# Channel attention: one product for numerator and denominator, paired row groups, rings of three banks

## The chip, the cores and the metric
The kernel runs on one NeuronCore of a Trainium2 chip. The metric is the device time of one execution in microseconds. The engines named here are TensorE (PE; PEld is its weight load), VectorE (DVE), ScalarE (ACT), GpSimd (POOL) and SyncE (SP, which only issues DMAs). PE writes to PSUM, which has eight banks of 512 float32 columns on 128 partitions.

## The reference, cut to what matters
The program is a decoder of twelve stages in float32 on x of shape (16, 128, 256): 16 batch elements of 128 tokens with 256 channels. Each stage is `x = layernorm(x + f(x))`. Stages 8 and 11 of the twelve are channel attention, and the change is in these two. The second multiplies the result by gamma.

```
def _L2_xattn_ref(q, k, v):          # x, ctx_2048, ctx_2048
    N_HEAD = 8
    qh = q.reshape(b * h, d // h, m)      # a head is 16 tokens; m = 256 channels
    kh = k.reshape(b * h, d // h, -1)
    vh = v.reshape(b * h, c // h, -1)
    qk = jnp.einsum('bdm,bdn->bmn', qh, kh) * scale       # 256 x 256 per head
    sm = jax.nn.softmax(qk, axis=-1)
    ret = jnp.einsum('bmn,bcn->bcm', sm, vh)
x = _layernorm(x + _L2_xattn_ref(x, ctx_2048, ctx_2048), axis=-1)
```

So for each of 16 batch elements and 8 heads there is a 256 by 256 softmax whose inner dimension is 16.

## The kernel before, in words
Every engine runs its own list of instructions in order, and semaphores (the `Signal` objects, `wait_ge` and `then_inc`) join them. A stage is a class; `Channels` is the first of the two, `ChannelsGamma` the second, with the same code. `Channels.order` (a generator) gives the order of steps to all engines: a loop over turns t, in which the steps work on different batch elements b, so that the stage is a pipeline over the 16 elements. Each engine's method goes through `order` and does its own share of a step.

The steps for one batch element b are these.
- "vt": PE turns the context (L2867, two 128 by 128 transposes), ACT copies it out as V (L2930), and POOL makes of it two masked copies VE, one for the even heads and one for the odd (L3023). POOL also makes XE (L3014) and KE (L3017), x and the context with the other heads' rows scaled to zero (parity e), and with one row of KE that lets a later constant be added.
- "s": PE computes scores (L2878) to find the largest of each row. A head pair lies on one group of 32 partitions, so a matmul has 32 rows, and four such matmuls can stand on the array's four row groups. The step is done for each half k of the 256 rows, into banks 0 to 3, and DVE takes the largest (L2967, four reductions).
- "sh": PE turns the largest values (L2887) and DVE puts them into the spare rows of XE (L2973). It uses bank 7, as "vt" does.
- "t": PE computes the scores again, turned and with the largest subtracted (L2899), four steps k on two row groups each, into banks 4 and 5; ACT takes the exponential (L2937) into E.
- "o": PE multiplies E with VE (L2912, hVE, the numerator, 16 matmuls) and then with ones masked in the same way (L2912, hone, the denominator, 8 and 8 matmuls), in four column groups, into bank 6. ACT copies the bank out (L2943).
- "mul": DVE takes the reciprocal over the full width of 256 columns (L2979), multiplies (L2982 or L2984) and adds x (L2987).
- "stats", "rsqrt", "scale": the layer norm of a group of four batch elements on DVE (`moments_of`, `rsqrt_of`, `scale_vector`).
- "aside": steps of the stage that comes next, placed in this stage's turns. For the second channel attention they belong to Quant (weights rounded; L2410, L2415 on PE in bank 7, L2516 to L2522 on DVE), in turns 3 to 16.

`room[n]` holds for each PSUM bank the signal that PE has to wait for before it writes the bank again. A float32 matmul shows in the trace as two records, so a step of 8 matmuls is "x16".

Of the kernel before, what the change touches and what calls it, by code (L numbers as in the profile page):

```python
# [2796 lines left out]
class Channels(Stage):  # L2797
# [6 lines left out]
    def weights(self):  # L2804
        c = self.c
        self.ctx, self.par, self.row, self.rp, self.gm = (
            c.f32("hctx", NB, D), c.f32("hpar", 2), c.f32("hrow", 2), c.f32("hrp", 2, 128), c.f32("hgm", 1))
# [6 lines left out]
    def load(self, sp):  # L2814
# [5 lines left out]
        self.fetch(sp, 4, (self.rp[:, :, :], i["c_rowpar"]), (self.gm[:, :], i["h_gamma"]))  # L2820
# [3 lines left out]
    def buffers(self):  # L2824
        c = self.c
        self.KE, self.XE, self.VE, self.V, self.MX, self.E, self.O = (c.sets(n, "h" + m, *z) for n, m, *z in (
            (3, "KE", 2, D), (3, "XE", 2, D), (3, "VE", 2, 2, 128), (2, "V", 2, 128), (2, "MX", 2, 128), (2, "E", 8, 2, D), (2, "O", 2, D)))
        self.R, self.P1 = [c.R, c.f32("hR", 4, D)], c.f32("hone", 2, 128)
        t, s, v, p = ((lambda name, n, e=e: self.sig(e, name, n)) for e in ("tensor", "scalar", "vector", "gpsimd"))
        self.ct, self.sc, self.sh, self.tr, self.o = t("ctx", 16), t("scores", 32), t("largest", 16), t("turned", 64), t("out", 16)  # L2830
        self.vk, self.ex, self.oc = s("v", 16), s("exp", 64), s("out", 16)
        self.row1, self.mx, self.xs, self.mul, self.sum = v("row", 1), v("max", 32), v("shift", 16), v("mul", 16), v("sum", 16)
        self.xe, self.ke, self.ve = p("xe", 16), p("ke", 16), p("ve", 16)
# [4 lines left out]
    def order(self):  # L2838

        yield "vt", 0, 0  # L2840
        for t in range(NB + 3):
            for step, b, k in (("sh", t - 1, 0), ("s", t, 0), ("mul", t - 3, 0), ("t", t - 1, 0), ("o", t - 2, 0), ("t", t - 1, 1), ("s", t, 1),
                               ("o", t - 2, 1), ("t", t - 1, 2), ("vt", t + 1, 0), ("o", t - 2, 2), ("t", t - 1, 3)):
                if 0 <= b < NB:
                    yield step, b, k
                if step == "s" and k == 1:
                    for n, first in (("stats", 6), ("rsqrt", 7), ("scale", 8)):
                        if t >= first and (t - first) % 4 == 0:
                            yield n, (t - first) // 4, 0
                    if t in self.ASIDE:  # L2850
# [762 lines left out]
```

## Time and profile before

| | us |
|---|---|
| median of 3 runs | 4110.23 |
| the three runs | 4107.7, 4110.23, 4121.14 |
| span of the profiled execution | 4117.8 |
| DVE busy in it | 3057.9 |
| ACT busy in it | 1939.7 |

The span is the time from the first to the last instruction of the one execution that was profiled; it lies within the range of the three runs' times. PE busy time is that of matmuls whose ends are modelled, so a busy PE is not a PE at its peak. Where an engine's row ends in square brackets, they say how long it had been idle before and who released it.

### The profile page before, as it was taken

To read this page: it belongs to the slowest core of one execution; us is meant where nothing else is said; L and a number is where in the kernel's file an instruction comes from. 1 tells how busy PE (TensorE), PEld (TensorE's weight loads), DVE (VectorE), ACT (ScalarE), POOL (GpSimd) and SP (SyncE) were. 2 spreads that over 40 slices of the span, in tenths; PEclk is the share of its full clock that TensorE was granted. 3 is DMA by queue.
4 is the path that set the end of the run, shared out by engine and by line. 5 is a ranking of instruction groups with operands and counts; after the bars stand their busy time and mean duration, and the time that the engine had idled before them with its cause. 6 is when DMAs were issued, how large, how long until landed. Compare 5 with 4: busy or idle time off the path is not lost. (4 is left out here: it accounts for less than half of the span.)

```text
span 4117.8 us, 65960 instructions
## 1 busy us (share of the span) xinstructions
PE 3583.7 (87%) x23747; PEld 2223.2 (54%) x23762; DVE 3057.9 (74%) x6508; ACT 1939.7 (47%) x4746; POOL 1167.6 (28%) x1208
## 2 busy tenths in 40 slices
PE   7799999998981777879999979888999999997885
PEld 3466666665661345645455545465655656564543
DVE  7788988988658675543455657868988898885678
ACT  4466666665532333311333324435656656563445
POOL 2533213334302000000111122114656555553210
PEclk9899999999995888889899988999999999997877
DMA  2222222222200100020000000022212211221000
GB/s 70 65 66 67 60 62 65 66 56 56 61 14 31 34 1 24 2 76 1 22 1 1 1 31 2 27 92 83 77 68 77 72 72 72 67 79 63 2 1 21
DMA packets 240594, 185.94 MB, mean 45 GB/s; under 512 B 117648, under 2 KB 216592, under 8 KB 239184
## 3 DMA queue, kind: packets, MB, share of 16 engines
q1 hardware_dynamic: 240272, 181.73, 14.7%
q8 instruction: 192, 3.15, 0.3%
q14 instruction: 130, 1.06, 0.1%
HBM read 166.45 MB, written 15.20 MB: 44 GB/s over the span
## 5 line engine op out<-in xcount | busy, mean ns | idle before, releaser
L310 PE MATMUL ps<-xT,min 128*128 128x512 f32 (+1 forms) x1072 | 503.0, 614 | 30.7 <-DVE macc L3349 30.3
L3349 DVE SCALAR_TENSOR_TENSOR macc<-ps,mcw,macc 128x508 f32<-128x508 f32 (+2 forms) x408 | 302.1, 741 | 81.2 <-ACT macc L3276 71.3
L3431 POOL TENSOR_TENSOR mSQ<-mSQ,mtn 128x512 f32<-128x512 f32 x128 | 240.2, 1877 | 362.1 <-ACT mtn L3301 362.0
L310 PEld LDWEIGHTS ps<-xT,min 128*128 128x128 f32 (+1 forms) x1072 | 191.9, 191 | 250.6 <-issue 204.3
L3424 POOL TENSOR_TENSOR mE<-mE,mCB 128x1024 f32<-128x1024 f32 x128 | 302.3, 2362 | 44.5 <-DVE mE L3359 26.5
L3359 DVE TENSOR_TENSOR_SCAN mE<-mE,mid 128x1024 f32<-128x1024 f32 x128 | 296.9, 2319 | 0.0
L3209 PE MATMUL ps<-mwo,macc 128*128 128x256 f32 x1024 | 244.5, 382 | 5.4 <-DVE macc L3366 5.3
L2937 ACT ACTIVATE hE<-ps 128x512 f32<-128x512 f32 x256 | 139.0, 595 | 223.5 <-PE ps L2899 223.5
L2351 POOL TENSOR_TENSOR lP<-lP,lm 128x512 f32<-128x512 f32 x64 | 66.6, 1041 | 574.5 <-DVE lm L2324 574.5
L3297 ACT ACTIVATE mtn<-ps,mcol 128x64 f32<-128x64 f32 x1024 | 222.9, 334 | 2.9 <-PE ps L3188 2.8
L826 POOL TENSOR_TENSOR dTB<-did,dNB 128x1024 f32<-128x1024 f32 (+1 forms) x10 | 28.7, 2869 | 662.6 <-DMA dNB<-d_N 598.4
L2260 ACT ACTIVATE lP<-ps,lm 128x128 f32<-128x128 f32 x256 | 90.6, 366 | 266.1 <-DVE lm L2320 266.1
L2967 DVE TENSOR_REDUCE hMX<-ps 128x2 f32<-128x512 f32 x256 | 158.8, 683 | 58.8 <-PE ps L2878 58.7
L3209 PEld LDWEIGHTS ps<-mwo,macc 128*128 128x128 f32 x1024 | 186.1, 192 | 28.7 <-DVE macc L3366 8.2
L732 DVE SCALAR_TENSOR_TENSOR dav<-ps,dsmall,dav 128x508 f32<-128x508 f32 (+2 forms) x192 | 142.3, 741 | 46.7 <-ACT dav L603 42.1
L2899 PE MATMUL ps<-hXE,hKE 32*128 32x256 f32 x1024 | 165.3, 445 | 12.9 <-DVE hXE L2973 7.9
L831 POOL TENSOR_TENSOR dTB<-dTB,dtmp 128x30 f32<-128x30 f32 (+11 forms) x300 | 168.7, 562 | 23.5
L732 DVE SCALAR_TENSOR_TENSOR daq<-ps,dsmall,daq 128x508 f32<-128x508 f32 (+2 forms) x192 | 142.3, 741 | 42.5 <-ACT daq L603 37.0
L830 POOL TENSOR_TENSOR dtmp<-dNB,dTB 128x30 f32<-128x30 f32 (+11 forms) x300 | 155.9, 520 | 23.5
L732 DVE SCALAR_TENSOR_TENSOR dak<-ps,dsmall,dak 128x508 f32<-128x508 f32 (+2 forms) x192 | 142.1, 740 | 25.3 <-ACT dak L603 20.7
L502 PE MATMUL ps<-dKQ 128*128 128x256 f32 x512 | 138.3, 397 | 25.9 <-ACT dO L678 17.3
L2161 PE MATMUL ps<-lCQ,lq 128*128 128x512 f32 (+1 forms) x256 | 142.6, 656 | 17.8 <-DVE lQA L2315 17.8
(581 smaller groups left out, 8470.9 us busy)
## 6 DMA issues: line engine op xcount, KB each, us to landing
mE<-m_decay SPq DMA_DIRECT2D x128, 512.0 KB, 3.6
dwk<-in_L_attn_Wk SPq DMA_DIRECT2D x64, 128.0 KB, 2.3
dwq<-in_L_attn_Wq SPq DMA_DIRECT2D x64, 128.0 KB, 2.4
dwv<-in_L_attn_Wv SPq DMA_DIRECT2D x64, 128.0 KB, 2.4
dwg<-in_L_attn_Wg SPq DMA_DIRECT2D x64, 128.0 KB, 2.4
dwo<-in_L_attn_Wo SPq DMA_DIRECT2D x64, 128.0 KB, 2.6
min<-in_m_in SPq DMA_DIRECT2D x2, 4096.0 KB, 18.5
d_N<-dNT SPq DMA_DIRECT2D x256, 16.0 KB, 1.5
```

Of the source, the lines that this page charges most:

```text
L310: t = pe.matmul(out, w[:, j, :], self.c.xT[:, j, blk(g, 512)], start=j == 0, stop=j == 1)
L732: x = dve.scalar_tensor_tensor(out=acc[:, :, 3 - j:T], in0=p[:, :, 0:T - 3 + j], scalar=small[:, 4 * k + j:4 * k + j + 1], in1=acc[:, :, 3 ...
L830: then(pool.tensor_tensor(part, bc(NB[:, s, s + 1:32], s, True), bc(TB[:, s, 0:s], 31 - s), ALU.mult))
L831: then(pool.tensor_tensor(low, low, part, ALU.subtract))
L2899: t = pe.matmul(bank(4 + i)[:, blk(lt, 256)], self.KE[x][r, e, blk(lt)], self.XE[x][r, e, :], start=True, stop=True)
L2967: m = dve.tensor_reduce(self.MX[y][:, k, 32 * r:32 * r + 32:16], bank(r).rearrange("p (e n) -> p e n", e=2), AX.X, ALU.max, negate=True)
L3209: t = pe.matmul(bank(to + j // 2)[:, blk(j % 2, 256)], self.acc[s][:, blk(j)], self.wo[:, i, :], start=i == 0 and j % 2 == 0, stop=i == 31 ...
L3297: x = act.activation(self.tn[s][:, h], bank(6)[:, h], ACT.Copy, scale=self.col[:, 4 * g + j, 2 * i + e:2 * i + e + 1])
L3349: x = dve.scalar_tensor_tensor(out=acc[:, :, 3 - j:T], in0=p[:, :, 0:T - 3 + j], scalar=self.cw[:, i, j:j + 1], in1=acc[:, :, 3 - j:T], op ...
L3359: dve.tensor_tensor_scan(E, E, self.id8[:, :, :].rearrange("p b t -> p (b t)"), 0.0, ALU.mult, ALU.add).then_inc(*self.de.up)
L3424: pool.tensor_tensor(E, E, bc(self.CB[g % 2][:, :, :].rearrange("p b t -> p (b t)"), 2), ALU.mult).then_inc(*self.em.up)
L3431: pool.tensor_tensor(self.SQ[g % 2][:, :], self.SQ[g % 2][:, :], self.tn[s][:, :], ALU.add).then_inc(*self.sqa.up)
```

## The change
It rewrites the stage's steps and their order.
- "vt" writes V straight into VE, 32 columns for each head pair and parity: 16 of V and 16 that are set to one at the stage's start. So "o" is one product of 16 matmuls whose output has the numerator on 16 partitions and the denominator on the next 16. POOL does nothing for V any more, and the masks are gone.
- A new step "ot": PE turns the copied result (four transposes into bank 6), so that numerators and denominators stand side by side in columns. DVE takes the reciprocal of 16 columns and multiplies with a broadcast into Y. A new step "back": PE turns Y back (two transposes into bank 7), and DVE adds x.
- "s" becomes four steps of two row groups, each behind the "t" step that uses the other two. Scores have the ring of banks 0, 1, 2 and turned scores that of banks 3, 4, 5; each bank is released by its own reduction or exponential. "vt" moves to bank 6.
- The pipeline is one turn deeper: "t" is now two turns behind "s" and "o" three. KE and XE have four buffers in place of three.
- The norm is cut into 13 small steps (`norm_step`) that stand between reductions of the turns after; the row statistics are taken one batch element at a time ("stat"). Asides stand at the end of a turn.

What PE's list holds for one turn in the first channel attention stage, before (hMX the largest, hKE and hXE the keys and queries, hE the exponentials, hctx the context):

```order
L2887 MATMUL ps<-ident_51,hMX_335_383 128x128 x2
L2878 MATMUL ps<-hKE_324_372,hXE_327_375 128x256 x8
L2899 MATMUL ps<-hXE_326_374,hKE_323_371 128x256 x4
L2912 MATMUL ps<-hE_336_384,hVE_331_379 32x256 x16
L2899 MATMUL ps<-hXE_326_374,hKE_323_371 128x256 x4
L2878 MATMUL ps<-hKE_324_372,hXE_327_375 128x256 x8
L2912 MATMUL ps<-hE_336_384,hone_389 32x256 x8
L2899 MATMUL ps<-hXE_326_374,hKE_323_371 128x256 x4
L2867 MATMUL ps<-ident_51,hctx_366 128x128 x2
L2912 MATMUL ps<-hE_336_384,hone_389 32x256 x8
L2899 MATMUL ps<-hXE_326_374,hKE_323_371 128x256 x4
```

And with the change (L2918 is the turned step, L2898 the score step, L2936 and L2943 the new turns of the result):

```order
L2918 MATMUL ps<-hXE_329_377,hKE_325_373 128x256 x4
L2898 MATMUL ps<-hKE_323_371,hXE_327_375 128x256 x4
L2906 MATMUL ps<-ident_51,hMX_332_380 128x128 x2
L2886 MATMUL ps<-ident_51,hctx_366 128x128 x2
L2918 MATMUL ps<-hXE_329_377,hKE_325_373 128x256 x4
L2898 MATMUL ps<-hKE_323_371,hXE_327_375 128x256 x4
L2929 MATMUL ps<-hE_334_382,hVE_330_378 32x256 x16
L2918 MATMUL ps<-hXE_329_377,hKE_325_373 128x256 x4
L2898 MATMUL ps<-hKE_323_371,hXE_327_375 128x256 x4
L2936 MATMUL ps<-ident_51,hO_336_384 128x128 x4
L2918 MATMUL ps<-hXE_329_377,hKE_325_373 128x256 x4
L2898 MATMUL ps<-hKE_323_371,hXE_327_375 128x256 x4
```

The two score steps of eight have become four of four, each behind a turned step; the denominator's two pieces are gone, and four transposes stand in front of the last pair (two more, L2943, follow it).

DVE's list for one turn of the change without norm steps, at the same place (hY the result before it is turned back, hrd the reciprocals):

```order
L3002 TENSOR_REDUCE hMX_332_380<-ps 128x2 x2
L3013 SCALAR_TENSOR_TENSOR hXE_327_375<-ps,hpar_367,hXE_327_375 128x256 x2
L3002 TENSOR_REDUCE hMX_332_380<-ps 128x2 x4
L3022 RECIPROCAL hrd_341_389<-ps 128x16
L3024 TENSOR_TENSOR hY_339_387<-ps,hrd_341_389 128x2x8x16
L3002 TENSOR_REDUCE hMX_332_380<-ps 128x2 x2
L3032 TENSOR_TENSOR R_57<-ps,X_49 128x256
L3009 BN_STATS st_58<-R_57 128x6
```

The shift stands between the first and second pair of reductions, the division between the third and fourth pair, and the add and the statistic behind the last.

The diff, cut to its core:

```diff
@@ order
-            for step, b, k in (("sh", t - 1, 0), ("s", t, 0), ("mul", t - 3, 0), ("t", t - 1, 0), ("o", t - 2, 0), ("t", t - 1, 1), ("s", t, 1),
-                               ("o", t - 2, 1), ("t", t - 1, 2), ("vt", t + 1, 0), ("o", t - 2, 2), ("t", t - 1, 3)):
+            for step, b, k in (("keys", t + 1, 0), ("stat", t - 5, 0), ("t", t - 2, 0), ("s", t, 0), ("sh", t - 1, 0), ("vt", t - 2, 0),
+                               ("t", t - 2, 1), ("s", t, 1), ("o", t - 3, 0), ("t", t - 2, 2), ("s", t, 2), ("ot", t - 3, 0),
+                               ("t", t - 2, 3), ("s", t, 3), ("back", t - 4, 0)):
@@ tensor
+            banks = [(8 * b + 2 * k + i) % 3 + (3 if step == "t" else 0) for i in range(2)]
...
-                for r in range(4):
-                    pe.wait_ge(*room[r])
+                for n in banks:
+                    pe.wait_ge(*room[n])
                 for e in range(2):
-                    for r in range(4):
-                        t = pe.matmul(bank(r)[:, blk(1 - e, 256)], self.XE[x][blk(r, 32), e, blk(k)], self.KE[x][blk(r, 32), e, :],
-                                      start=True, stop=True)
+                    for i, n in enumerate(banks):
+                        r = blk(2 * (1 - k % 2) + i, 32)
+                        t = pe.matmul(bank(n)[:, blk(1 - e, 256)], self.XE[x][r, e, blk(k // 2)], self.KE[x][r, e, :], start=True, stop=True)
                 t.then_inc(*self.sc.up)
-                for r in range(4):
-                    room[r] = self.mx.at(2 * b + k + 1)
+                for i, n in enumerate(banks):
+                    room[n] = self.mx.at(8 * b + 2 * k + i + 1)
...
-                for e in ((0, 1), (0,), (1,))[k]:
+                for e in range(2):
                     for lt in range(2):
                         for r in range(4):
-                            w = self.P1[:, e, blk(r, 32)] if k else self.VE[x][:, lt, e, blk(r, 32)]
-                            t = pe.matmul(bank(6)[blk(r, 32), blk(min(k, 1), 256)], w, self.E[y][:, 2 * r + e, lt, :], start=e + lt == 0,
-                                          stop=e + lt == 2)
+                            t = pe.matmul(bank(6)[blk(r, 32), blk(e, 256)], self.VE[y][:, lt, r, e, :], self.E[y][:, 2 * r + e, lt, :],
+                                          start=lt == 0, stop=lt == 1)
+            elif step == "ot":
+                pe.wait_ge(*room[6])
+                for n in range(4):
+                    t = pe.transpose(bank(6)[:, blk(n)], self.O[y][:, blk(n)], c.ident[:, :])
+                t.then_inc(*self.ot.up)
+                room[6] = self.mul.at(b + 1)
+            elif step == "back":
+                pe.wait_ge(*room[7])
+                pe.wait_ge(*self.mul.at(b + 1))
+                for qt in range(2):
+                    t = pe.transpose(bank(7)[:, blk(qt)], self.Y[y][:, blk(qt)], c.ident[:, :])
+                t.then_inc(*self.bk.up)
+                room[7] = self.sum.at(b + 1)
@@ vector
-                for r in range(4):
-                    m = dve.tensor_reduce(self.MX[y][:, k, 32 * r:32 * r + 32:16], bank(r).rearrange("p (e n) -> p e n", e=2), AX.X, ALU.max,
-                                          negate=True)
-                m.then_inc(*self.mx.up)
+                for i in range(2):
+                    n, r = (8 * b + 2 * k + i) % 3, 32 * (2 * (1 - k % 2) + i)
+                    dve.tensor_reduce(self.MX[y][:, k // 2, r:r + 32:16], bank(n).rearrange("p (e n) -> p e n", e=2), AX.X, ALU.max,
+                                      negate=True).then_inc(*self.mx.up)
+                    late, w = (b - 8) % 4, 2 * k + i - 1
+                    if b >= 8 and w >= 0 and 7 * late + w <= 12:
+                        self.norm_step(dve, own, (b - 8) // 4, 7 * late + w)
...
-                r = own(dve.reciprocal(q, q))
+                r = own(dve.reciprocal(rd, p[:, :, :, 1, 0]))
                 dve.wait_ge(own.sem, r)
+                dve.tensor_tensor(self.Y[y][:, :].rearrange("p (w e c) -> p e w c", e=2, c=16), p[:, :, :, 0, :],
+                                  rd.unsqueeze(3).broadcast_to([128, 2, 8, 16]), ALU.mult).then_inc(*self.mul.up)
```

## Rows read from the trace of the kernel before

**Rows 1.** Page, part 1: busy us (share of the span) x instructions

```profile
PE 3583.7 (87%) x23747; PEld 2223.2 (54%) x23762; DVE 3057.9 (74%) x6508; ACT 1939.7 (47%) x4746; POOL 1167.6 (28%) x1208
```

**Rows 2.** Timeline of a plain turn: start, us, engine, line, operation, count, [idle]

```profile
2517.64 1.15 PE L2878 MATMUL ps<-hKE,hXE 32*128 32x256 f32 x16
2517.75 0.88 DVE L2973 SCALAR_TENSOR_TENSOR hXE<-ps,hpar,hXE 128x256 f32<-128x256 f32 x2 [2.19 <-PE ps L2887]
...
2518.68 1.13 PE L2899 MATMUL ps<-hXE,hKE 32*128 32x256 f32 x8
...
2518.86 2.48 DVE L2967 TENSOR_REDUCE hMX<-ps 128x2 f32<-128x512 f32 x4 [0.23 <-PE ps L2878]
...
2519.74 1.93 PE L2912 MATMUL ps<-hE,hVE 128*32 128x256 f32 x32
...
2521.61 0.48 PE L2899 MATMUL ps<-hXE,hKE 32*128 32x256 f32 x2
...
2521.63 0.48 PE L2878 MATMUL ps<-hKE,hXE 32*128 32x256 f32 x2
...
2521.93 0.38 PE L2899 MATMUL ps<-hXE,hKE 32*128 32x256 f32 x2
...
2523.53 1.07 PE L2912 MATMUL ps<-hE,hone 128*32 128x256 f32 x16
...
2525.60 0.44 PE L2867 MATMUL ps<-ident,hctx 128*128 128x128 f32 x2
...
2525.96 1.07 PE L2912 MATMUL ps<-hE,hone 128*32 128x256 f32 x16
...
2528.03 0.44 PE L2887 MATMUL ps<-ident,hMX 128*128 128x128 f32 x2
```

**Rows 3.** Groups by line and shape, 2455 to 2668: busy us, mean ns of one

```profile
L2967 DVE TENSOR_REDUCE hMX<-ps 128x2 f32<-128x512 f32 x128 | 79.4, 683 | 22.3 <-PE ps L2878 22.3
L2979 DVE RECIPROCAL hO<-hO 128x256 f32<-128x256 f32 x16 | 27.9, 1741 | 0.4 <-ACT hO L2943 0.4
...
L2987 DVE TENSOR_TENSOR R<-R,X 128x256 f32<-128x256 f32 x8 | 3.4, 425 | 0.3
...
L246 DVE TENSOR_SCALAR X<-hR,st,rsq 128x256 f32<-128x256 f32 x8 | 2.8, 406 | 0.0
...
L196 DVE TENSOR_SCALAR rsq<-st 128x4 f32<-128x4 f32 x4 | 0.6, 160 | 0.0
...
L2937 ACT ACTIVATE hE<-ps 128x512 f32<-128x512 f32 x128 | 69.5, 594 | 105.9 <-PE ps L2899 105.9
```

**Rows 4.** First score step, turns of the largest in both stages, and their groups

```profile
2457.52 2.09 PE L2878 MATMUL ps<-hKE,hXE 32*128 32x256 f32 x16 [10.35 <-POOL hKE L3017]
...
2495.76 0.44 PE L2887 MATMUL ps<-ident,hMX 128*128 128x128 f32 x2
...
L2887 PE MATMUL ps<-ident,hMX x32: 272/328/474, 2467.2 to 2641.0; 128*128 128x128 f32 x32
...
3798.85 0.44 PE L2887 MATMUL ps<-ident,hMX 128*128 128x128 f32 x2
...
L2887 PE MATMUL ps<-ident,hMX x32: 272/328/475, 3769.6 to 3971.9; 128*128 128x128 f32 x32
```

**Rows 5.** Timeline of the second stage, a numerator and a context turn

```profile
3851.05 3.63 PE L2912 MATMUL ps<-hE,hVE 128*32 128x256 f32 x32
...
3862.05 0.66 PE L2867 MATMUL ps<-ident,hctx 128*128 128x128 f32 x2 [3.38 <-DVE qg L2522]
```

**Rows 6.** Stretches: us, PE busy, PEld, DVE, ACT, POOL, granted clock, DMA

```profile
2480.00:2485.00 5.00, 5.00 (x32) 3.41 (x31) 1.58 (x4) 1.09 (x2) 3.14 (x6) 0.50 0.00 0
...
2490.00:2495.00 5.00, 5.00 (x64) 2.88 (x60) 2.48 (x4) 2.60 (x6) 0.04 (x1) 1.00 0.00 0
```

**Rows 7.** Timeline of the first stage, a turn with a norm

```profile
2552.50 1.13 PE L2899 MATMUL ps<-hXE,hKE 32*128 32x256 f32 x8 [1.45 <-DVE hXE L2973]
...
2553.57 3.22 PE L2912 MATMUL ps<-hE,hVE 128*32 128x256 f32 x32
```

More of the change, by code:

```diff
@@ L2844, in order @@
                 if 0 <= b < NB:
                     yield step, b, k
[L2846 to L2850, printed above, removed]
-                        yield "aside", *self.ASIDE[t]
-        yield "rsqrt", 3, 0
-        yield "scale", 3, 0
+            if t in self.ASIDE:
+                yield "aside", *self.ASIDE[t]
@@ new lines, in order, with norm_step @@
+            if t == NB:
+                yield "norm", 2, 0
+        yield "stat", NB - 1, 0
+        yield "norm", 3, 0
+    def norm_step(self, dve, own, g, k):
+        c, (y, v, a) = self.c, self.sw
+        dve.wait_ge(own.sem, self.last)
+        if k == 0:
+            for j in range(4):
+                self.last = own(dve.bn_aggr(c.st[:, j, 6:8], c.st[:, j, 0:6]))
+        elif k == 1:
+            self.last = own(dve.tensor_scalar(v, c.st[:, :, 7:8].rearrange("p a b -> p (a b)"), 1e-5, None, ALU.add))
+        elif k == 2:
+            self.last = own(dve.tensor_scalar(y.bitcast(I32), v.bitcast(I32), -0.5, 1597463007.0, ALU.mult, ALU.add))
+        elif k == 12:
+            c.scale_vector(dve, g, self.R[g % 2])
+        elif k % 3 == 0:
+            self.last = own(dve.scalar_tensor_tensor(out=a, in0=y, scalar=-0.5, in1=y, op0=ALU.mult, op1=ALU.mult))
+        elif k % 3 == 1:
+            self.last = own(dve.tensor_tensor(a, a, v, ALU.mult))
+        else:
+            self.last = own(dve.scalar_tensor_tensor(out=y, in0=a, scalar=1.5, in1=y, op0=ALU.add, op1=ALU.mult))
@@ L2893, in tensor @@
                     pe.wait_ge(*self.xs.at(b + 1))
-                for i in range(2):
-                    pe.wait_ge(*room[4 + i])
+                for n in banks:
+                    pe.wait_ge(*room[n])
                 for lt in range(2):
-                    for i in range(2):
+                    for i, n in enumerate(banks):
                         r = blk(2 * rr + i, 32)
-                        t = pe.matmul(bank(4 + i)[:, blk(lt, 256)], self.KE[x][r, e, blk(lt)], self.XE[x][r, e, :], start=True, stop=True)
+                        t = pe.matmul(bank(n)[:, blk(lt, 256)], self.KE[x][r, e, blk(lt)], self.XE[x][r, e, :], start=True, stop=True)
@@ L2998, in gpsimd @@
+                a.then_inc(*self.sum.up)
+            elif step == "norm":
+                for n in range(13):
+                    self.norm_step(dve, own, b, n)
     def gpsimd(self, pool, own):
```

125 lines of the change are left out of this document (59 added, 66 removed).

## The prediction

> **What bounds the kernel now.** I read four views. First the page's busy line: over the whole program TensorE (PE) is busy 87% and VectorE (DVE) 74% [rows 1]. The change touches only the two channel-attention stages, so I looked for those: by the rows of L2887 their largest scores are turned from 2467.2 to 2641.0 us and from 3769.6 to 3971.9 us [rows 4]. Second, the timeline of one undisturbed turn of the loop (one batch element) [rows 2]. PE starts something every microsecond and its rows show no wait: score step 1.04 us (2517.64 to 2518.68), turned-score step 1.06, numerator 1.87, turned step beside score step 1.92, first half of the denominator and a turned step 2.07, context turn 0.36, second half and a turned step 2.07, turn of the largest 0.37 (as the context turn): 10.76 us. A turned step taken at 1.06, half the denominator is 1.0. DVE does 8 reductions in it (two of 2.48), the shift 0.88, a reciprocal of 1.74 and two elementwise passes of 0.42 [rows 3]: 8.4, with waits between. So PE bounds a plain turn. Third, groups by line for the costs. Fourth, the pace: the third turn of the largest stands at 2495.76 and the last at 2641.0, so 13 turns at 11.17 us; in the second stage 3798.85 to 3971.9, 13 at 13.31 [rows 4]. The second is slower from two things: PE waits for DVE before the context turn, 3.38 us in one row, because Quant's small steps share bank 7 with it, and the clock then falls, so that a numerator takes 3.63 us in place of 1.93 [rows 5].
>
> **Removed.** The denominator's matmuls (L2912 with hone): two pieces of 1.00, 2.0 us of PE per turn. The full-width reciprocal, 1.74, and one elementwise pass. GpSimd's masking of V goes too; no row of PE waits for it, so it is worth nothing.
>
> **Moved.** Score steps become four of two row groups, each behind a turned step on the other two. Rows 2 price that: a step on two groups (8 records) takes as long as one on four (16 records), about 1.05, and at 2521.61 and 2521.63 the turned step and the score step on the idle groups start together. So a pair should cost 1.06, and four pairs 4.24, where before the same work took 1.04 + 1.06 + 1.92 + 1.07 + 1.07 = 6.16 us. Saved: 1.9 us. This is the largest uncertainty on PE; the other end is no overlap, 1.92 for each pair (the time of turned plus score step before), 7.7 in all.
>
> The Trainium skill speaks against it: "TensorE: Matmul & The Clock Gate", Part 3, says that matmuls are strict FIFO in start and end and only weight loads are pulled ahead. By that rule a pair costs near 1.9. The trace disagrees: the later score matmuls at 2521.63 start 0.3 us ahead of the turned step's second two at 2521.93 [rows 2]. I go by the rows and keep the rule as a rival.
>
> **Added.** On PE: four turns of the result and two back. Two turns take 0.36 to the next step; four cost between 0.36 and 0.73, I take 0.6; with the context turn and the turn of the largest now together (0.6): 0.6 + 0.6 + 0.36 = 1.56 against 0.73. PE's sum is 4.24 + 1.87 + 1.56 = 7.7 us a turn against 10.76.
> On DVE: a 16-column reciprocal out of PSUM, between the 0.16 of a 4-column operation and the full-width 1.74; the count of columns puts it near the first, 0.2. A multiply with a broadcast and the result reordered: between 0.42 (L2987) and twice that; I take 0.48 as for L2973, which also reads PSUM. The add from PSUM 0.48, one row statistic 0.4 (an elementwise pass over the same 256 columns). DVE per turn: 8 reductions in pairs 5.2 (0.62 apart, the last 0.68), shift 0.88, these four 1.56, and the group norm over four turns (4 aggregates, 11 small operations of about 0.2 with their waits, four scalings of 0.41) 1.0: 8.6.
> On ACT: 8 exponentials of 0.59 and two copies, of 512 and 256 columns, at 0.6 or less: 5.9. Hidden, unless a turn falls under that.
>
> **The new wait.** The score ring has three banks: score step k+1 needs the first reduction of step k. PE queues its instructions in order, so behind a waiting score step stand the next product and everything after. I walked one turn with the durations above, 0.07 from PE to DVE and 0.05 back [rows 2]; times from the first score step: complete 1.15, first reduction 1.90, second step 1.95 to 3.0; product to 4.85 (DVE is idle from 4.8 to 6.1 here: nothing but the third pair can feed it); third pair to 5.9; turn of the result; its first reduction ends 6.75, fourth pair 6.8 to 7.85; DVE does reciprocal and multiply before the fourth pair's reductions, first of these ends 8.8; next turn begins 8.85. DVE is then still at the last reduction, the add and the statistic until 10.3, which puts the next first reduction 0.25 late. So 9.1 a plain turn: neither engine is full, the alternation binds. The norm's small operations between reductions cost about 0.5 and the four scalings 1.6 once per group; averaged 0.5. 9.6, and 0.2 for what the walk misses: **9.8** in the first stage against 11.17. In the second, 2.14 (13.31 - 11.17) is added by Quant's steps and the clock. They now stand at the turn's end and bank 7 no longer holds up the product, but the 2-us activations on ACT and the reductions on DVE stay; I keep about half, 1.15: **10.95**.
>
> **The clock.** PE runs at 1.2 GHz (0.50) at each stage's start: at 2480 to 2485 busy 5.00 of 5.00 with score and turned steps and still 0.50; 1.00 from 2490 on, when the first products are running [rows 6]. The first product now comes a turn later. At half clock a score step takes 2.1; four of them with a wait of 0.7 each make turns of about 11.7, and the third turn of the largest comes 36.9 us after the first score step, where it came 38.2 after [rows 4]: 1.3 earlier. The next turn, at half clock until its product ends, I put at 13.6. Extra memsets (two of 512 columns) hold up GpSimd's first keys by 0.75.
>
> **The end.** The pipeline is one turn deeper; the last two turns have turned steps only, and the last product, result turn, add and norm follow one another. Against them, before, ran the last divisions. By the same durations +3 us, and +5 in the second stage, where the rows fall to half clock.
>
> **Sum.** First stage: 13 x 11.17 = 145.2 becomes 13.6 + 12 x 9.8 = 131.2: -14.0. Second: 173.0 becomes 13.6 + 12 x 10.95 = 145.0: -28.0. Starts 2 x (-1.3 + 0.75) = -1.1. Ends +8. Together -35 us. The profiled execution has a span of 4117.8, the median of the three runs is 4110.23; they differ by 0.2%, and the difference carries over: 4110 - 35 = **4075 us**. About 12 us (0.3%) is what a measurement of this kernel tells from no change.
>
> **Rivals.**
> 1. *The second stage's stalls vanish wholly*: 9.8 there too, 12 x 1.15 = 14 more, and a little on the walk: 4056. For: the wait on Quant's chain in front of the context turn goes. Against: the ACT and DVE work of it stays. 0.16.
> 2. *The handoffs eat it*: eight handoffs per turn, each 0.15 dearer than in the walk: 1.2 a turn, 24 turns, 29 us: 4104, no change. For: every step now starts behind such a handoff, where few did. Against: the two kinds seen in rows 2 took 0.07 and 0.05. 0.13.
> 3. *The clock, and slower.* A wait of 1.45 us for the shift was followed by a product of 3.22 us in place of 1.93: PE fell to the lower clock [rows 7]. After the change PE is idle or waiting about 1.9 of 9.6 us in every turn, in pieces of 0.3 to 0.5, with only one product in it to bring the clock back. At half clock the turn is 4 x 2.1 + 3.6 + 2.5 (eight turns) + 0.8 = 15.3, 5.5 more. The gain of 35 is gone when 6 more of 24 turns run so; with half of them, -35 + 66: 4141. For: PE is no longer continuously busy. Against: the gaps are small, the pairs denser, and a drop before was healed by one product. 0.15.
> 4. *The skill's order rule holds*: PE's sum 7.7 + 3.4 = 11.1, the turn 11.9: 2.1 x 24 = 50 more: 4125. 0.05.
> My forecast, 4062 to 4098: 0.51.
>
> **Range and chances.** Under 4098: forecast 0.51, rival 1 0.16, a part of rival 2: faster 0.69. Within 12 us: 0.13. Slower: rivals 3 and 4, less their mild ends: 0.18. The range reaches from somewhat under rival 1, 4040, to 4112, which takes in rival 2 and leaves the slower cases out; 4062 to 4098 is the forecast's own.
>
> **What would show it.** Turned step and score step should start within 0.05 us of each other and a pair last about 1.1; plain turns 9.1 us apart; DVE idle during the product; waits of PE on the reductions of 0.3 to 1 us; no wait of over 1 us in front of the context turn near 3850; clock as before. Pairs of 1.9 us would prove the order rule; a clock of 0.5 in many turns rival 3; plain turns of over 10.3 with full clock rival 2.

## The result and the profile after

The changed kernel takes **4058.51 us** (median of 4 runs, 4055.63 to 4060.61) against 4108.97 for the kernel before (4 runs, 4097.44 to 4121.14, three of them those of the table ahead of the prediction): ratio 0.9869, 95% interval 0.9846 to 0.9891, faster by 1.3%. Forecast were 4075, with a range of 4040 to 4112. The profiled executions have spans of 4117.8 and 4057.2, 60.6 apart; the medians are 50.5 apart, because the execution of before that was profiled took longer than its median. The parts below are parts of the 60.6.

The page's busy line after, which answers to [rows 1]:

```profile
PE 3510.4 (87%) x22915; PEld 2198.7 (54%) x22930; DVE 3001.8 (74%) x6502; ACT 1939.4 (48%) x4746; POOL 1125.0 (28%) x1144
```

The shares did not move, though PE lost 73 us of work: they are averages over twelve stages, of which two changed. The plain turn shows more. This is its timeline after (start, us, engine, line, operation, count, idle before), and it answers to [rows 2]. L2898 is a score step, L2918 a turned step, L2929 the product, L2936 the turn of the result, L2943 the turn back, L2906 the turn of the largest, L3002 the reductions.

```profile
2530.85 0.44 PE L2906 MATMUL ps<-ident,hMX 128*128 128x128 f32 x2
2530.96 1.29 DVE L3002 TENSOR_REDUCE hMX<-ps 128x2 f32<-128x512 f32 x2
...
2531.44 0.70 PE L2918 MATMUL ps<-hXE,hKE 32*128 32x256 f32 x4
...
2531.80 0.48 PE L2898 MATMUL ps<-hKE,hXE 32*128 32x256 f32 x2
...
2532.86 1.93 PE L2929 MATMUL ps<-hE,hVE 128*32 128x256 f32 x32
2532.96 1.29 DVE L3002 TENSOR_REDUCE hMX<-ps 128x2 f32<-128x512 f32 x2
2534.72 0.48 PE L2918 MATMUL ps<-hXE,hKE 32*128 32x256 f32 x2
2534.75 0.48 PE L2898 MATMUL ps<-hKE,hXE 32*128 32x256 f32 x2
...
2535.04 0.38 PE L2918 MATMUL ps<-hXE,hKE 32*128 32x256 f32 x2
2535.07 0.38 PE L2898 MATMUL ps<-hKE,hXE 32*128 32x256 f32 x2
...
2535.81 0.66 PE L2936 MATMUL ps<-ident,hO 128*128 128x128 f32 x4
...
2535.99 1.29 DVE L3002 TENSOR_REDUCE hMX<-ps 128x2 f32<-128x512 f32 x2 [1.74 <-PE ps L2898]
2536.64 0.48 PE L2918 MATMUL ps<-hXE,hKE 32*128 32x256 f32 x2 [0.17 <-ACT hE L2969]
2536.83 0.48 PE L2898 MATMUL ps<-hKE,hXE 32*128 32x256 f32 x2
...
2537.90 0.44 PE L2943 MATMUL ps<-ident,hY 128*128 128x128 f32 x2
...
2539.90 0.44 PE L2906 MATMUL ps<-ident,hMX 128*128 128x128 f32 x2
```

From 2530.85 to 2539.90 a turn takes 9.05 us, where it took 10.76. In the pair behind the product, turned step and score step run interleaved, 0.03 us apart, and the whole pair goes from 2534.72 to 2535.81: 1.09. In the other three pairs the score step starts 0.36, 0.19 and 0.29 us behind its turned step (the first two are shown, at 2531.80 and 2536.83), and they take 1.42, 1.25 and 1.35 us. Each of these three score steps starts 0.15 us after the end of the first reduction of the score step before it (the one that starts at 2530.96 ends at 2531.65). This is the wait for the ring's third bank. No row shows it as idle time, because PE is busy with the turned step meanwhile.

DVE waits once, 1.74 us: it has reduced every score bank that was filled, and PE is at the product, so nothing feeds it. That is the place the prediction's walk put it at. PE is idle 0.2 us twice a turn, for the exponential of ACT.

The groups by line and shape from 2455 to 2648 (busy us, mean ns | idle before) answer to [rows 3]:

```profile
L3002 DVE TENSOR_REDUCE hMX<-ps 128x2 f32<-128x512 f32 x128 | 83.4, 687 | 49.8 <-PE ps L2898 48.9
...
L3024 DVE TENSOR_TENSOR hY<-ps,hrd 128x256 f32<-128x256 f32 x16 | 6.8, 424 | 0.5
L3022 DVE RECIPROCAL hrd<-ps 128x16 f32<-128x16 f32 x16 | 4.0, 250 | 4.1 <-PE ps L2936 4.1
L3009 DVE BATCH_NORM_STATS2 st<-R 128x6 f32<-128x256 f32 x8 | 3.4, 428 | 0.3
```

The reciprocal costs 0.25 where it cost 1.74, the multiply 0.42, the statistic 0.43. The first score step of each stage and the turns of the largest, which answer to [rows 4]:

```profile
2455.67 1.22 PE L2898 MATMUL ps<-hKE,hXE 32*128 32x256 f32 x4 [11.32 <-POOL hKE L3057]
...
2493.42 0.47 PE L2906 MATMUL ps<-ident,hMX 128*128 128x128 f32 x1
2503.68 0.44 PE L2906 MATMUL ps<-ident,hMX 128*128 128x128 f32 x2
2618.50 0.44 PE L2906 MATMUL ps<-ident,hMX 128*128 128x128 f32 x2
3744.43 1.19 PE L2898 MATMUL ps<-hKE,hXE 32*128 32x256 f32 x3 [14.92 <-issue]
3779.35 0.33 PE L2906 MATMUL ps<-ident,hMX 128*128 128x128 f32 x1
3917.70 0.44 PE L2906 MATMUL ps<-ident,hMX 128*128 128x128 f32 x2
```

The third turn is at 2493.42 and the last at 2618.50: 13 turns take 125.08, 9.62 us each, where they took 11.16. In the second stage 13 take 138.35, 10.64 each against 13.30. (The last turns of before start at 2640.80 and 3971.73; the 2641.0 and 3971.9 that end the groups of [rows 4] are the second matmuls of these turns.) The 60.6 us by parts (the end is counted to the end of the stage's last scaling):

| us against before | first stage | second stage |
|---|---|---|
| the first keys | +0.75 | +0.75 |
| first score step to third turn | -0.5 | -4.0 |
| 13 turns | -20.0 | -34.5 |
| end | +3.0 | -6.1 |

Together -60.6. The ten other stages differ too, by -2.6 us ahead of the first of the two stages, +3.1 between them and -0.5 behind the second, which cancel.

The second stage gained 14.5 us more than the first. Its clock is a part of that, as the stretches of the 13 turns show, before and after (us, PE busy, PEld, DVE, ACT, POOL, granted clock, DMA):

```profile
3798.85:3971.73 172.88, 158.63 (x1723) 93.08 (x1721) 130.58 (x252) 76.87 (x137) 47.61 (x76) 0.88 0.01 2
3779.35:3917.70 138.35, 119.06 (x1376) 77.74 (x1374) 105.20 (x236) 76.60 (x139) 28.38 (x47) 0.96 0.01 2
```

The waits for bank 7 in these turns fell from 8.9 to 5.9 us. How the 14.5 splits between the two, and what the context's move to bank 6 did by itself, no run separates.

The clock rose later in the first stage than before, as forecast, yet it cost less. Stretches after (us, PE busy, PEld, DVE, ACT, POOL, granted clock, DMA), and they answer to [rows 6]:

```profile
2475.00:2495.00 20.00, 17.28 (x104) 12.07 (x104) 10.00 (x17) 6.17 (x12) 2.01 (x4) 0.50 0.00 1
2515.00:2535.00 20.00, 19.21 (x248) 12.64 (x244) 15.45 (x30) 11.12 (x23) 4.01 (x8) 1.00 0.01 2
2495.00:2500.00 5.00, 5.00 (x68) 2.83 (x60) 2.12 (x5) 1.99 (x4) 0.00 (x0) 0.82 0.02 3
...
3774.00:3776.00 2.00, 1.34 (x18) 0.99 (x18) 1.28 (x3) 1.17 (x3) 0.00 (x0) 1.00 0.00 0
```

In the first stage the clock is 0.50 until 2495 and rises within the first product, which takes 2.07 us; the plain turns run at 1.00. In the second it is at 1.00 from 3774 on. The first product of each stage, in the timeline of PE:

```profile
2496.50 2.07 PE L2929 MATMUL ps<-hE,hVE 128*32 128x256 f32 x32
...
3781.36 1.93 PE L2929 MATMUL ps<-hE,hVE 128*32 128x256 f32 x32
```

Not all turns are plain. Where the group norm's four scalings stand, a turn of the first stage is 10.6 to 10.8 us and the one behind it 10.2 to 10.9, and PE waits (this answers to [rows 7], with the wait shorter but the fall of the clock the same: the product behind it takes 3.48 for 1.93):

```profile
2559.62 0.44 PE L2906 MATMUL ps<-ident,hMX 128*128 128x128 f32 x2 [1.32 <-DVE hR L3032]
2561.92 3.48 PE L2929 MATMUL ps<-hE,hVE 128*32 128x256 f32 x32
```

In the second stage, Quant's small steps stand at the turn's end. This is one of them, and the turned step three microseconds later (it answers to [rows 5]):

```profile
3820.23 0.27 PE L2410 MATMUL ps<-ident,qg 128*1 128x128 f32 x1 [1.40 <-DVE R L3030]
...
3823.37 0.80 PE L2918 MATMUL ps<-hXE,hKE 32*128 32x256 f32 x2
```

The wait is shorter than the 3.38 of before, but it is not gone: PE waits until DVE's add (L3030) has read bank 7, and behind it the matmuls take 0.80 in place of 0.48, the lower clock.

### The profile page after: what moved, and what is told of

Its sections match the earlier page's. It is cut to its first block and busy times, and to the rows that moved or that the text cites. A ratio compares the mean times of both kernels' runs of the same rounds, so it can differ in the third digit from the quotient of the medians.

```text
span 4057.2 us, 64282 instructions
## 1 busy us (share of the span) xinstructions
PE 3510.4 (87%) x22915; PEld 2198.7 (54%) x22930; DVE 3001.8 (74%) x6502; ACT 1939.4 (48%) x4746; POOL 1125.0 (28%) x1144
## 3 DMA queue, kind: packets, MB, share of 16 engines
q14 instruction: 129, 1.06, 0.1%
## 5 line engine op out<-in xcount | busy, mean ns | idle before, releaser
L3002 DVE TENSOR_REDUCE hMX<-ps 128x2 f32<-128x512 f32 x256 | 166.7, 687 | 100.7 <-PE ps L2898 98.9
L2898 PE MATMUL ps<-hKE,hXE 32*128 32x256 f32 x1024 | 170.9, 455 | 40.3 <-issue 14.9
L2918 PE MATMUL ps<-hXE,hKE 32*128 32x256 f32 x1024 | 154.4, 419 | 20.7 <-ACT hE L2969 18.6
L502 PE MATMUL ps<-dKQ 128*128 128x256 f32 x512 | 137.6, 396 | 25.7 <-ACT dO L678 16.9
```

Of the source, the lines that this page charges most:

```text
L2898: t = pe.matmul(bank(n)[:, blk(1 - e, 256)], self.XE[x][r, e, blk(k // 2)], self.KE[x][r, e, :], start=True, stop=True)
L2918: t = pe.matmul(bank(n)[:, blk(lt, 256)], self.KE[x][r, e, blk(lt)], self.XE[x][r, e, :], start=True, stop=True)
L3002: dve.tensor_reduce(self.MX[y][:, k // 2, r:r + 32:16], bank(n).rearrange("p (e n) -> p e n", e=2), AX.X, ALU.max, negate=True).then_inc(* ...
```

## The experiments

All times are medians; "before" is the kernel before, run beside the group of runs that shares its median. It varies by 14 us between the groups, so runs of different groups are compared by their ratios. "Plain turn" is the distance of two turns of the largest in the first stage; it was 10.76 before.

| run | us | before | ratio, 95% interval | plain turn |
|---|---|---|---|---|
| the changed kernel | 4058.51 | 4108.97 | 0.9869, 0.9846 to 0.9891 | 9.05 |
| e1 same row groups | 4134.57 | 4107.58 | 1.0077, 1.0047 to 1.0107 | 11.11 |
| e2 wait for both reductions | 4124.08 | 4107.58 | 1.0054, 1.0033 to 1.0074 | 10.85 |
| e3 product twice | 4105.82 | 4107.58 | 1.0008, 0.9990 to 1.0026 | 10.78 |
| e4 before, less denominator | 4111.03 | 4107.58 | 1.0018, 1.0000 to 1.0037 | 10.24 |
| e5 extra work beside the product | 4070.3 | 4114.25 | 0.9895, 0.9864 to 0.9925 | 9.06 |
| e6 the same on the chain | 4117.97 | 4114.25 | 1.0014, 1.0005 to 1.0024 | 10.47 |
| e7 norm in one block | 4073.91 | 4114.25 | 0.9917, 0.9894 to 0.9940 | 9.05 |
| e8 small steps inside the turn | 4046.6 | 4114.25 | 0.9847, 0.9824 to 0.9869 | 9.05 |
| e9 small steps ahead of back | 4062.81 | 4100.77 | 0.9903, 0.9885 to 0.9920 | 9.05 |
| e10 inside, scalings apart | 4036.45 | 4100.77 | 0.9839, 0.9825 to 0.9852 | 9.05 |
| e11 e10, back ahead of the product | 4058.53 | 4100.77 | 0.9897, 0.9883 to 0.9912 | 9.65 |

**e1. The score step on the row groups of its turned step.**

```diff
-                        r = blk(2 * (1 - k % 2) + i, 32)
+                        r = blk(2 * (k % 2) + i, 32)
```

> The changed kernel, with each score step on the same two row groups as the turned step ahead of it (before it was on the other two). Same instructions, same order, same waits. Theory A (the row groups let the two steps run beside each other, and the turn is a chain of PE and DVE): each of the four score steps starts about 0.8 us later, the plain turn goes from 9.06 to 12.2 us, the program to about 4130 us. Rival (matmuls keep strict program order in the array whatever the groups, the gain comes only from the denominator that is gone): no change, 4058 us.

Timeline of PE in it:

```profile
2531.19 1.13 PE L2918 MATMUL ps<-hXE,hKE 32*128 32x256 f32 x8
2532.16 1.03 PE L2898 MATMUL ps<-hKE,hXE 32*128 32x256 f32 x8
2533.12 0.44 PE L2943 MATMUL ps<-ident,hY 128*128 128x128 f32 x2
```

On the same two groups the score step starts 0.97 behind the turned step and the pair takes 1.93, not 1.09. Four pairs take 7.7 us in place of 5.1, and the turn is 11.11, 2.06 longer; 0.4 of the 2.6 goes into the two waits for the exponential, which are gone. The expectation had 12.2 for the turn, because it priced all four pairs as the one behind the product; its time, 4130, came near, with more turns at the low clock in the second stage (13 of them take 184.5 us). The whole gain is gone, and more. So without the pairing of row groups the change does not pay. With it falls rival 4. The Trainium skill, "TensorE: Matmul & The Clock Gate", Part 3, says that matmuls never pass one another in start or end; here the third and fourth records of the turned step start at 2535.04, behind the score step's first at 2534.75, which stands later in PE's list. The Trainium skill's "TensorEngine Tiling (Array Packing)", Key Properties, says that different tiles can run matmuls in parallel, and with this e1 and the changed kernel agree: 1.93 on the same groups, 1.09 on different ones.

**e2. The score step waits for both reductions of the one before,** as with two banks in place of three.

```diff
                 for n in banks:
                     pe.wait_ge(*room[n])
+                if b or k:
+                    pe.wait_ge(*self.mx.at(8 * b + 2 * k))
```

> The changed kernel, but each score step waits for both reductions of the step before it, so that the third bank of the ring gives nothing. Theory A (chain of alternation binds): 0.55 to 0.62 us more at each of four steps, 2.4 us a turn, plain turn about 11.4 us, program about 4120 us. Rival (PE's sum of work binds and the waits fall into slack): under 0.5 us a turn, program under 4072 us.

A pair in the timeline of PE:

```profile
2538.38 1.13 PE L2920 MATMUL ps<-hXE,hKE 32*128 32x256 f32 x8
2539.56 1.13 PE L2900 MATMUL ps<-hKE,hXE 32*128 32x256 f32 x8
```

The turn grows by 1.8 us, and the whole gain is lost by one wait. It shows in no row as a long wait of PE but in pairs that come apart. In all of them but the one behind the product, the score step starts 0.8 to 1.2 us behind its turned step (here 2538.38 and 2539.56) and runs mostly alone. So three of the four pairs need the third bank of the ring. The expectation, 2.4 us a turn, was 0.6 too high.

**e3. The product computed twice,** the second over the first.

```diff
-                for e in range(2):
+                for e in (0, 1, 0, 1):
```

> The changed kernel with the 16 matmuls of the product issued twice into the same place, so PE does what it did when the denominator had its own, 1.87 us more a turn. Theory A: the product stands in the chain while DVE idles, so the whole 1.87 shows, plain turn 10.9 us, program about 4116 us. Rival (DVE's work of 8.6 us a turn binds now): most of it hides, plain turn under 9.8, program under 4080.

The product takes 3.66 in place of 1.93 and the turn 10.78 in place of 9.05: each 1.73 more. So the product lies wholly on the path, and DVE's slack beside it hides none of it. 32 turns x 1.73 = 55; by the ratios the program rose by 0.0139, 57 us.

**e4. The kernel before with half of the denominator's matmuls left out** (the denominators then lack part of their terms).

```diff
-                for e in ((0, 1), (0,), (1,))[k]:
-                    for lt in range(2):
+                for e in ((0, 1), (), (0, 1))[k]:
+                    for lt in range(1 if k else 2):
```

> The kernel before, with half of the denominator's matmuls left out (8 of 16 per batch element, so its sums are over half the rows), 1.0 us less of PE a turn; all else as before. Theory A (PE's sum bound the turn before): plain turn from 10.76 to about 9.8 us, 32 turns, 25 to 30 us less, program about 4080 us. Rival (DVE or the alternation bound the turn before as well, and only the new order brings the gain): turn stays over 10.5, program within 8 us of the kernel before.

Timeline of PE in it, a plain turn:

```profile
2530.47 1.13 PE L2899 MATMUL ps<-hXE,hKE 32*128 32x256 f32 x8 [0.41 <-ACT hE L2937]
```

1.0 us of PE's work was taken out and the turn fell by 0.52; the rest is now a wait for the exponential. The turns with a norm got longer (14.3 and 15.7, before 13.95 and 12.81), and of the time nothing was gained. My theory had 4080 and missed. Less work on PE alone brought nothing here: the order of work had to change too. So the prediction's sentence that PE bounds a plain turn of before holds for half a microsecond of the 1.0 only. This run does not separate how much of the loss is the norm and how much the clock, which is 0.86 in the second stage's 13 turns where it was 0.88.

**e5 and e6. An extra full-width reciprocal of 1.74 us on DVE,** in e5 behind the second pair of reductions (`k == 1`), in e6 behind the third (`k == 2`).

```diff
+                if k == 1:
+                    own(dve.reciprocal(self.wide[:, :], c.X[:, b, :]))
```

> The changed kernel with one full-width reciprocal (1.74 us, x into a scratch tile that nobody reads) added on DVE to each batch element, placed right behind the second pair of reductions, where DVE idles 1.74 us during the product. Theory A (the turn is a chain, DVE has one hole in it): hidden, plain turn within 0.15 us of 9.06, program under 4070 us; a little where asides or norm fill the hole. Rival (DVE's sum binds): all of it shows, plain turn 10.8, program about 4110.

> The same reciprocal, one position later: behind the third pair of reductions, ahead of the division and the fourth pair. Same work as the run beside it. Theory A: it stands on the chain, all 1.74 us show, plain turn 10.8 us, program about 4108 us. Rival (DVE's sum binds): the same time as the run beside it, wherever that lies.

Timeline of DVE, in e5:

```profile
2537.95 1.74 DVE L3009 RECIPROCAL hwide<-X 128x256 f32<-128x256 f32 x1
2539.77 1.29 DVE L3003 TENSOR_REDUCE hMX<-ps 128x2 f32<-128x512 f32 x2
```

and in e6:

```profile
2538.77 1.29 DVE L3003 TENSOR_REDUCE hMX<-ps 128x2 f32<-128x512 f32 x2 [1.74 <-PE ps L2899]
2539.97 1.74 DVE L3009 RECIPROCAL hwide<-X 128x256 f32<-128x256 f32 x1
```

In e5 it fills exactly the 1.74 us in which DVE was idle, and plain turns stay at 9.06. In e6 DVE has the idle time and the work one behind the other, and turns take 10.47: 1.41 of the 1.74 show, not all of it as expected. The same instructions, one place apart: 48 us by the medians. In the profiled executions the first stage's 13 turns are 20 us longer in e6 and the second's 31, where the granted clock is 0.91 in e5 and 0.80 in e6; so a part of the 48 is the clock. Nor is e5 free over the whole program: 4070.3 is 0.3 above what was expected, and the second stage's 13 turns take 143.4 us in place of 138.35, with the clock at 0.91 in place of 0.96. This shows what bounds the kernel after: a chain that goes from PE to DVE and back, on which DVE's work counts except beside the product.

**e7. The norm's 13 steps in one block** after a turn's last reduction, in place of one between two reductions.

```diff
-                    if b >= 8 and w >= 0 and 7 * late + w <= 12:
-                        self.norm_step(dve, own, (b - 8) // 4, 7 * late + w)
+                    if b >= 8 and late == 1 and k == 3 and i == 1:
+                        for w in range(13):
+                            self.norm_step(dve, own, (b - 8) // 4, w)
```

> The changed kernel with the 13 norm steps of the first two groups of each stage done in one block behind the last reduction of a turn, not one by one between the reductions of two turns. The kernel before lost 3.2 us and a piece of full clock in such turns. Theory A: one turn in four gets about 4 us longer and loses some clock, the other one gets its 1.6 back; 3 to 4 us more per group, four groups, program about 4072 us. Rival (spreading the norm carries most of the gain, since leaving out half the denominator alone brought nothing): 4085 us or more.

PE in a turn with the block:

```profile
2559.56 0.69 PE L2906 MATMUL ps<-ident,hMX 128*128 128x128 f32 x2 [3.72 <-DVE hR L3033]
```

The turn with the norm is 12.84 in place of 10.64, PE waits 3.72 in place of 1.32. Spread out, the norm is worth some 13 us in the turns (the 13 of the first stage take 130.3 in place of 125.1, those of the second 145.7 in place of 138.35); the ratios' intervals are barely apart. The expected time was met, but not the way to it: the turn behind the block takes 10.23 and later 11.90 us, and does not come down to a plain one.

**e8. Quant's small steps behind the second score step,** where they stood before, in place of the turn's end.

```diff
                     yield step, b, k
-            if t in self.ASIDE:
-                yield "aside", *self.ASIDE[t]
+                if step == "s" and k == 1 and t in self.ASIDE:
+                    yield "aside", *self.ASIDE[t]
```

> The changed kernel with the next stage's steps (asides) back at the place they had before, behind the second score step, not at the turn's end. Theory A (the place is what freed PE from waiting for Quant's chain): second stage 10 to 15 us longer with waits of PE of 2 us or more near the four turns of wturn and wall, first stage unchanged, program about 4070 us. Rival (context turns having left bank 7 is what freed it): under 4 us, 4060 us.

I had put it down as a part of the gain that they moved to the end; the sign was wrong. The second stage's 13 turns fall to 128.1 us (10.64 each becomes 9.85). The ratios' intervals of this run and of the changed kernel overlap, so it is the turns that show the gain. The timeline of PE there, the same small step:

```profile
3798.38 0.27 PE L2410 MATMUL ps<-ident,qg 128*1 128x128 f32 x1 [0.15 <-DVE hXE L3013]
3798.58 1.93 PE L2929 MATMUL ps<-hE,hVE 128*32 128x256 f32 x32
```

0.15 in place of 1.40, and the product behind it runs at the full clock. Two theories were left: bank 7 (the small step follows the turn back, whose reader on DVE is late), or DVE's own work for the small step at a bad place.

**e9. The small steps one place earlier,** ahead of "back" in place of behind it.

```diff
+                if step == "back" and t in self.ASIDE:
+                    yield "aside", *self.ASIDE[t]
                 if 0 <= b < NB:
                     yield step, b, k
-            if t in self.ASIDE:
-                yield "aside", *self.ASIDE[t]
```

> The changed kernel with Quant's small steps one place earlier than at a turn's end: ahead of the step back instead of behind it. Theory A (the bank): PE's small step there writes bank 7, and behind the turn back it must wait until DVE's add has read that bank (waits of 1.40 to 1.64 us, four times, in the changed kernel's second stage, and the clock falls behind one of them). Ahead of the turn back the bank's last reader is the shift, long done: the four waits go, 13 turns of the second stage fall from 138 to about 129 us, the span from 4057 to about 4048, near the 4046 of the kernel with the small steps behind the second score step. Theory B (DVE's queue): what costs is the small step's own work on DVE at the end of a turn, which this move leaves there: second stage 136 to 138 us, span about 4056.

PE and DVE in the second stage:

```profile
3803.66 0.27 PE L2410 MATMUL ps<-ident,qg 128*1 128x128 f32 x1
...
3804.97 0.27 DVE L2516 TENSOR_REDUCE qg<-ps 1x1 f32<-1x128 f32 x1
...
3805.30 0.52 PE L2943 MATMUL ps<-ident,hY 128*128 128x128 f32 x2 [1.37 <-DVE qg L2516]
```

The waits of the small steps went, as theory A said, and came back on the other side: now the turn back waits until DVE has read the small step's result out of bank 7, four times, 6.6 us in all, up to 2.05. No gain (13 turns 140.0 against 138.35). The time alone does not tell the two theories apart, since B had 136 to 138. The waits do: each of them ends with DVE's read of what the step ahead wrote into bank 7. So the bank is the cause, but not through the one neighbour that I named. When two steps of PE that use bank 7 stand next to each other, the second waits until DVE, which has the last score step's two reductions to do first, has read what the first wrote. In e8 the step ahead in bank 7 is the turn of the largest, whose shift is nearly done (0.15), and the turn back comes two pairs later. No run gives the small steps a bank of their own.

**e10. e8, and the four scalings as four separate norm steps.**

```diff
-        elif k == 12:
-            c.scale_vector(dve, g, self.R[g % 2])
+        elif k >= 12:
+            j = k - 12
+            x = dve.tensor_scalar(c.X[:, 4 * g + j, :], ...)
```

> The changed kernel with the small steps behind the second score step and the group norm's last step, four scalings of 0.41 us in a row (1.6 us between two reductions), taken apart into four norm steps, each between two reductions. Theory A (DVE's work on the chain costs its whole length, beside the product nothing): a turn with scalings, 10.6 to 10.9 us in the first stage, falls by 0.8 to 1.2, since some of the four come to lie where DVE is idle; and the waits of 1.3 to 1.4 us of PE for them go with the clock's falls: 3 turns in each stage, 6 x 1.2 = 7 us: about 4039 where the small steps alone gave 4046.6. Rival (the sum of DVE's work counts, wherever it stands): no change, 4046.

```profile
2561.80 0.44 PE L2910 MATMUL ps<-ident,hMX 128*128 128x128 f32 x2 [0.53 <-DVE hR L3036]
```

The turn with the scalings is 9.82 in place of 10.64 and the one behind it 9.25 in place of 10.89; the first stage's 13 turns take 121.1 against 125.1 us, the second's 125.5 against 128.1 in e8. The rival, that only DVE's sum counts, falls. The turns of both stages together are 6.7 us shorter than in e8, where 7 were expected. The best of all kernels here, 4036.45: 1.6% under before, by ratio 0.9839. Against e8, 0.9847, the intervals overlap; the turns in the trace, not the medians, show the gain.

**e11. e10 with "back" and its statistic ahead of the product.**

```diff
-                               ("t", t - 2, 1), ("s", t, 1), ("o", t - 3, 0),
+                               ("t", t - 2, 1), ("s", t, 1), ("back", t - 4, 0), ("stat", t - 4, 0), ("o", t - 3, 0),
```

> As the one with the small steps inside and the scalings apart, and besides the turn back, its add and its statistic stand ahead of the product instead of at the turn's end (they are a turn older there). Theory A: the add (0.42) and the statistic (0.43) then follow the second pair of reductions, beside the product, where DVE is idle for about 1.7 us; the last score step's reductions reach the next turn sooner, and the pipeline's end is one step shorter: 0.25 us a plain turn, 24 turns, 6 us: about 4033. Rival: the turn back ahead of the product makes PE wait for the multiply of the turn before or lengthens the product's start by 0.44: no gain, or 2 to 5 us lost.

```profile
2534.72 0.44 PE L2946 MATMUL ps<-ident,hY 128*128 128x128 f32 x2 [0.42 <-DVE hXE L3016]
...
3795.72 0.44 PE L2946 MATMUL ps<-ident,hY 128*128 128x128 f32 x2 [1.14 <-DVE qg L2516]
```

Slower than e10 by 0.6%, 22 us: the rival's direction, but it had 2 to 5. In the first stage the turn back now waits for the shift, the last reader of bank 7, in nearly every turn, and holds up the product behind it; plain turns are 9.65, and 13 turns take 127.5 us in place of 121.1. The larger part lies in the second stage, 137.6 in place of 125.5. There the edit does a second thing: the small steps, which in e10 had two pairs between them and the turn back, now stand right ahead of it, and four times it waits 1.14 to 1.47 us for DVE's read of the small step, as in e9. The add does lie in DVE's idle time now, so that alone is no gain when the step that feeds it stands on PE's side of the chain. How the 0.6 us of a plain turn splits between this wait and those for the exponentials (0.59 before a turned step) I did not resolve.

## Why the prediction was right, and where its sizes were off

4058.5 lies within the stated range of 4040 to 4112, but under the 4062 to 4098 that the forecast called its own.

**The pair** was the largest uncertainty: 1.06 forecast, 1.09 measured behind the product, where both steps start together. The other three take 1.42, 1.25 and 1.35, so four cost 5.1 and not 4.24. The turn does not pay for that: counted from the score step's start, each of the three still takes 1.06 to 1.07, as in the walk, and the turned step's earlier start lies in what would be waiting. e1 shows that the gain hangs on the overlap.

**The plain turn**: 9.1 by the walk, 9.05 measured, with DVE idle for 1.74 during the product. The walk's reasons hold: e3 and e6 show the product and DVE's work behind it on the chain, e5 the slack beside the product. The waits on the reductions are there as well, but they hold the score step back by 0.2 to 0.4 us only, and beside the turned step, where a row of PE does not show them as idle; the walk had the next turn begin when the first of the last reductions ends, and so it does. Only the handoff from DVE to PE is dearer, 0.15 in place of 0.05. The waits of 0.2 us for ACT's exponential ahead of a turned step, which the walk left out, do not lengthen the turn, since the score step behind has to wait for its reduction anyway.

**The averaged turn of the first stage**: 9.8 forecast, (2618.50 - 2503.68) / 12 = 9.57 measured. The 0.2 "for what the walk misses" was not needed.

**The turn with the clock's rise**: 13.6 forecast, 10.26 measured in the first stage and 9.05 in the second. This is the term of the turns whose size was most wrong. I let the whole product run at half clock; the clock rose within it, and it took 2.07 us in place of some 3.6. In the second stage the clock even rose before any product (1.00 from 3774 on, the first product at 3781.36), with PE busy 1.34 of 2 us, so its first product runs in a plain turn; why there and not in the first stage, no run tells.

**The second stage**: 10.95 forecast, (3917.70 - 3788.40) / 12 = 10.78 measured. I kept half of Quant's cost, for the ACT and DVE work of its steps, and said that bank 7 no longer holds up the product. That reason was wrong: four waits of 1.40 to 1.65 us for bank 7, 5.9 in all, stayed, and behind one of them the clock fell for 3.4 us. In e8, where these waits are 0.9 in all, the last 12 turns take 9.89 against 9.56 in the first stage: the ACT and DVE work that I kept 1.15 for costs some 0.3. That the forecast's size came out near was luck.

**The ends**: +3 in the first stage, as measured. In the second +5 was forecast and -6.1 measured: before, the last steps ran at half clock (0.55 in 3980 to 4000), after mostly at full (0.91 in 3918 to 3938). I had carried the low clock of before over to a kernel whose end is laid out differently.

**The starts**: +0.75 for the memsets as forecast; -0.5 and -4.0 in place of twice -1.3.

**The sum**: -35 forecast, -50.5 by the medians, -60.6 by the profiled executions. The 25.5 between the first and the last are the turn of 13.6 (3.3 and 4.6), the other turns (12 at 0.23 and 12 at 0.17: 4.9), the ends (11.1) and the starts (1.9), less 0.3 for the last turns of before, which the prediction took to start 0.2 us later than they do. So the ends and the turn with the clock's rise, two terms about the low clock, are three quarters of the miss.

**The rivals.** Rival 1, that the second stage's stalls vanish wholly, gave 4056 and came near the time for other reasons; the stalls are there. Rival 2 falls: a plain turn takes 9.05 and not 10.3, though the handoff from DVE to PE does cost 0.1 more than in the walk. Rival 3: the clock does fall, in two turns of the first stage behind waits of 1.3 and 1.4 us, and in two turns of the second, but in no plain turn, and over the whole program it is 0.934 against 0.928. Rival 4 falls by e1.

## What to carry to other kernels

Once two engines hand work to and fro, price the chain and not either engine's sum: walk one turn with durations from the trace, look where each engine idles, and put side work there (48 us lay between two places for the same instruction, a part of it by the clock). Before a step is moved, list who uses its PSUM bank before and after it: here a small step next to another user of the bank cost 5.9 to 6.6 us, whichever of them stood first, and 0.9 two pairs away from it. Work that is taken off the busiest engine may bring nothing by itself: of 1.0 us a turn in e4, half was lost to the next limit at once, and the rest elsewhere.

## What the runs showed of the hardware

- Float32 matmuls with 32 rows on two row groups, and later ones on the two others, run side by side on PE: two steps of 4 matmuls (8 records) each take 1.09 us when both can start together, on the same groups 1.93. The later step's first starts 0.29 us ahead of the earlier step's third record.
- The granted clock fell behind waits of PE of 1.32, 1.41, 1.40 and 1.46 us, and a product of 1.93 us then took 3.48. Behind four other waits in the second stage, of 1.33 to 1.65 us, it did not fall. It rose within a product in the first stage, and before any product in the second.
- A matmul that had to wait for a reduction started 0.15 us after the reduction's end, in all three such pairs of a plain turn.
- A reciprocal of 128x16 out of PSUM takes 250 ns and one of 128x256 in SBUF 1741; as an estimate from these two, 6.2 ns for each further column.
